# Float16 halves of the attention weights, and probabilities times values as three fp32r products

## What is computed

```python
def _fp8_linear_pertensor(x, wq, w_scale, in_scale):
    xq = _div_clamp_fp8(x, in_scale)          # clip, bf16, then float8 e4m3
    return einsum('bsi,oi->bso', xq * in_scale, wq) * w_scale
def _gqa(q, k, v):                            # q: 16 heads of 128, k and v: 8 groups
    scores = einsum('bsghd,btgd->bghst', q, k) / sqrt(128)
    return einsum('bghst,btgd->bsghd', softmax(scores), v)
...
q, qx = ln(linear(x, wq)), ln(linear(x, wqx))
k, v = ln(linear(x, wk)), linear(x, wv)
kx, vx = split(ctx @ w_kv_x.T); kx = ln(kx)
out = linear(concat(_gqa(q, k, v), _gqa(qx, kx, vx)) * smooth, wproj)
x = x + tanh(g) * out
```

## Time and profile before

| | |
|---|---|
| median of 3 runs | 1677.27 us (1674.27 to 1680.37) |
| profiled execution, span | 1673.7 us; the page gives no other time of it |
| TensorE busy | 1623.2 us, 97% |
| ScalarE busy | 1102.9 us, 66% |
| VectorE busy | 1083.2 us, 65% |
| GpSimd busy | 485.3 us, 29% |
| moved by DMA | 220.7 MB |

### The profile page before, as it was taken

The page is one execution under the profiler, slowest core; times in us unless marked ns, Lnnn a source line. Parts: engine busy times, 40 slices in busy tenths (PEclk is TensorE's granted clock), DMA queues, the critical chain, the costliest instruction groups (busy, mean ns, idle before and its releaser), DMA issues.

```text
span 1673.7 us, 27163 instructions
## 1 busy us (share of the span) xinstructions
PE 1623.2 (97%) x9136; PEld 1335.0 (80%) x9136; DVE 1083.2 (65%) x2115; ACT 1102.9 (66%) x2983; POOL 485.3 (29%) x515
## 2 busy tenths in 40 slices
PE   7989989999999999999999999999999999999998
PEld 6878756666778888888788888888888788887887
DVE  6258855445985767777777776566666666788322
ACT  4364245553559888888888887878778787885100
POOL 1001122224424424334243343342433433330000
PEclk9999989999999999999999999999999999999999
DMA  7031649995772143283342362121152121110011
GB/s 271 26 107 41 258 151 325 311 316 187 243 270 80 54 183 104 92 333 109 113 182 89 133 264 83 57 88 57 57 218 79 44 108 56 38 45 1 25 38 38
DMA packets 75156, 220.72 MB, mean 132 GB/s; under 512 B 6368, under 2 KB 14560, under 8 KB 68640
## 3 DMA queue, kind: packets, MB, share of 16 engines
q1 hardware_dynamic: 69360, 200.61, 33.1%
q0 software_dynamic: 5680, 18.62, 3.6%
HBM read 158.65 MB, written 60.56 MB: 131 GB/s over the span
## 4 chain that ended last, share of the span: by engine, by line
PE 78%; DVE 4%; ACT 4%; issue 1%; DMA 1%; POOL 1%; ACTq 0%; POOLq 0%; SPq 0%; DVEq 0%
PE bank L2478 10%; PE bank L2479 10%; PE bank L97 7%; PE bank L2541 7%; PE bank L99 7%; PE bank L98 7%; PE bank L2559 6%; PE bank L2572 6%; PE bank L2530 5%; PE bank L1388 4%; PE bank L1408 4%; PE bank L2551 3%; PE bank L1368 1%; DVE x_res L1747 1%; ACT t_sc L2699 1%
## 5 line engine op out<-in xcount | busy, mean ns | idle before, releaser
L2810 DVE TENSOR_TENSOR t_hn<-bank,t_rs 128x256 f32<-128x256 f32 (+1 forms) x256 | 130.7, 552 | 140.1 <-POOL t_rs L2443 72.7
L2478 PE MATMUL bank<-t_slot,t_x_q 128*128 128x512 f32 x512 | 205.8, 402 | 0.0
L2440 POOL TENSOR_SCALAR t_ve<-t_ss 128x4 f32<-128x4 f32 (+1 forms) x128 | 25.9, 202 | 616.4 <-DVE t_ss L2806 608.9
L2479 PE MATMUL bank<-t_slot,t_x_q 128*128 128x512 f32 x512 | 200.2, 391 | 0.0
L2699 ACT ACTIVATE t_sc<-bank,t_mx 128x128 f32<-128x128 f32 x512 | 183.9, 455 | 3.5 <-DVE t_mx L2830 3.5
L2443 POOL TENSOR_TENSOR t_rs<-t_ve,t_mhalf 128x4 f32<-128x4 f32 (+1 forms) x128 | 171.0, 1336 | 10.6
L2699 ACT ACTIVATION_READ_ACCUMULATOR t_sc<-bank,t_mx 128x1 f32 x512 | 151.6, 296 | 0.0
L2737 ACT ACTIVATE t_y<-bank,smooth 128x128 bf16<-128x128 f32 x512 | 139.3, 401 | 1.9 <-PE bank L2559 1.9
L2541 PEld LDWEIGHTS bank<-t_hT 128*128 128x128 f32 x1024 | 120.1, 191 | 16.8 <-ACT t_hT L2726 16.2
L2541 PE MATMUL bank<-t_hT 128*128 128x128 f32 x1024 | 131.0, 281 | 2.3 <-ACT t_hT L2726 2.3
L2479 PE MATMUL bank<-t_slot,t_x_kv 128*128 128x256 f32 x512 | 125.6, 283 | 0.0
(11 more groups left out here) (344 smaller groups left out, 4159.1 us busy)
## 6 DMA issues: line engine op xcount, KB each, us to landing
t_slot<-w_ready SPq DMA_DIRECT2D x16, 2048.0 KB, 9.8
t_xh<-xq_scratch SPq DMA_DIRECT2D x64, 512.0 KB, 3.6
t_cr<-in_ctxT_dram SPq DMA_DIRECT2D x64, 256.0 KB, 2.7
y_rows<-s_y SPq DMA_DIRECT2D x39, 256.0 KB, 3.2
e_w<-in_w_units_dram SPq DMA_DIRECT2D x8, 1024.0 KB, 12.4
w_rows<-in_w_qkv_dram SPq DMA_DIRECT2D x8, 1024.0 KB, 6.2
w_ready<-w_hi SPq DMA_DIRECT2D x8, 1024.0 KB, 6.3
w_ready<-w_lo SPq DMA_DIRECT2D x8, 1024.0 KB, 6.1
```

Of the source, the lines that this page charges most:

```text
L2478: nc.tensor.matmul(out, x_in[:, k, :], w[0][:, k, a:b], start=k == 0, stop=False)
L2479: last = nc.tensor.matmul(out, x_in[:, k, :], w[1][:, k, a:b], start=False, stop=k == KT - 1)
L2810: nc.vector.tensor_tensor(hn[:, lo:hi, :], b3[bk][:, 0:hi - lo, :], rs[:, lo:hi].unsqueeze(2).broadcast_to([P, hi - lo, P]), ALU.mult).the ...
```

## The change

Each weight half of the segments q, qx, v and k is stored in float16 (`w_half`), those of the context segment stay float32 (`w_plain`). So that float16 can hold them, each segment is divided by a power of two: `half_constants()` in `Retention` finds it from the scales (an input `scales` of 1 MB is loaded for it), and `env.sigma` keeps the factor that undoes it, which ScalarE applies in the squares, the values and the keys. Queries and keys read the float16 rows `xh` directly, `rows_q` and `rows_kv` go. Probabilities and values get a high half (float32r, by ScalarE as before) and a low half by VectorE (`probs_low`, `values_low`), and `attend` is `three_products`. `w_lo` has one buffer instead of two, and stores are two for each half. The diff, cut to its core:

```diff
 class ReadyWeights:
+    STORED = 32
     def store_hi(self, sp, n):
         sp.dma_start(self.dram[quarter, :, :, 0, k, :].rearrange("s p n -> p s n"),
-                     self.hi[:].bitcast(FP32).rearrange("p (s n) -> p s n", s=4)).then_inc(self.hi_st, 16)
+                     self.hi[:].rearrange("p (s n) -> p s n", s=3)).then_inc(self.hi_st, 16)
+        sp.dma_start(self.dram_plain[quarter, :, 0, k, :], self.hi_rest[:].bitcast(FP32)).then_inc(self.hi_st, 16)
...
+        def half_constants():
+            ins, steps = env.cols("in_scale"), self.halves
+            dve.wait_ge(self.scales_in, 16)
+            v.tensor_reduce(self.most[:], self.scales[:], op=ALU.max, axis=AX.X, apply_absolute_value=True
+                            ).then_inc(steps, 1)
...
         low(2)
+        half_constants()
         added(1)
...
     def sync(sp):
         def x_rows(m):
             if m >= 2:
-                sp.wait_ge(xkv_in, m - 1)
-                sp.wait_ge(xq_in, m - 1)
+                sp.wait_ge(b_ps, (m - 1) * 2)
         def weights(quarter, seg, loaded):
+            home = homes[quarter][seg]
+            if seg == KVX:
+                sp.dma_start(slots[home][:].bitcast(FP32), ready.dram_plain[quarter]).then_inc(loaded, 16)
+            else:
+                sp.dma_start(halves16[home][:], ready.dram[quarter, {KV: 2, WQ_: 0, WQX: 1}[seg]]).then_inc(loaded, 16)
...
     def tensor(pe):
-        def project(out, w, a, b, x_in):
+        def project(out, w, a, b, rows, kind):
             for k in range(KT):
-                nc.tensor.matmul(out, x_in[:, k, :], w[0][:, k, a:b], start=k == 0, stop=False)
-                last = nc.tensor.matmul(out, x_in[:, k, :], w[1][:, k, a:b], start=False, stop=k == KT - 1)
+                nc.tensor.matmul(out, rows[:, k, kind, :], w[0][:, k, a:b], start=k == 0, stop=False)
+                last = nc.tensor.matmul(out, rows[:, k, kind, :], w[1][:, k, a:b], start=False, stop=k == KT - 1)
             return last
...
         def attend(m, par):
             for part in range(2):
-                pe.wait_ge(pt_in, m * 2 + part + 1)
+                pe.wait_ge(ptl_in, m * 2 + part + 1)
                 for g in range(QG):
-                    h = (1 - part) * QH + 2 * g
-                    last = nc.tensor.matmul(bank[6 + part][:, g * 256:(g + 1) * 256],
-                                            vv[par][:, (1 - part) * QG + g, :], pT[:, h:h + 2, :],
-                                            start=True, stop=True)
+                    h, v = (1 - part) * QH + 2 * g, (1 - part) * QG + g
+                    last = three_products(nc, bank[6 + part][:, g * 256:(g + 1) * 256], vv[par][:, v, :],
+                                          vv_lo[par][:, v, :], pT[:, h:h + 2, :], pT_lo[:, h:h + 2, :], True, True)
                 last.then_inc(pv_ps, 1)
...
     def scalar(act):
-        def rows_kv(m, par):
-            nc.scalar.activation(x_kv[:], xh[par][:, :, 2:4, :].rearrange("p k v s -> p v k s"), ACT.Copy
-                                 ).then_inc(xkv_in, 1)
-        def rows_q(m, par):
-            nc.scalar.activation(x_q[:], xh[par][:, :, 0:2, :].rearrange("p k v s -> p v k s"), ACT.Copy
-                                 ).then_inc(xq_in, 1)
...
-                nc.scalar.activation(hn[:, part * QH:part * QH + QH, :], b3[part][:], ACT.Square).then_inc(sqb_in, 1)
+                nc.scalar.activation(hn[:, part * QH:part * QH + QH, :], b3[part][:], ACT.Square,
+                                     scale=env.sigma[:, part:part + 1]).then_inc(sqb_in, 1)
...
     def vector(dve):
+        def values_low(m, par):
+            dve.wait_ge(vcp_in, m * 2 + 2)
+            if later(m, 2):
+                dve.wait_ge(pv_ps, m * 2 - 2)
+            nc.vector.scalar_tensor_tensor(vv_lo[par][:, 0:QG, :], b3[2][:, 2:4, :], env.sigma[:, 3:4],
+                                           vv[par][:, 0:QG, :].bitcast(FP32), ALU.mult, ALU.subtract)
+            nc.vector.tensor_tensor(vv_lo[par][:, QG:2 * QG, :], b3[3][:, 2:4, :],
+                                    vv[par][:, QG:2 * QG, :].bitcast(FP32), ALU.subtract)
+        def probs_low(m):
+            for part in range(2):
+                dve.wait_ge(pt_in, m * 2 + part + 1)
+                if part == 0 and later(m, 1):
+                    dve.wait_ge(pv_ps, m * 2)
+                nc.vector.tensor_tensor(pT_lo[:, side(part), :], b3[6 + part][:], pT[:, side(part), :].bitcast(FP32),
+                                        ALU.subtract).then_inc(ptl_in, 1)
...
             if has(i):
                 normalise_b(i)
+            if has(i - 1):
+                probs_low(i - 1)
             if has(i + 1):
                 sums_a(i + 1)
...
             if has(i + 1):
+                values_low(i + 1, 1 - par)
                 normalise_a(i + 1)
...
         def last_steps():
             normalise_b(M - 1)
             de.x_lo(dve, 0, range(2, KT))
+            probs_low(M - 2)
             rounded(M - 3, 1 - M % 2, 1)
...
             de.h_low(dve, 0, 1)
+            probs_low(M - 1)
             rounded(M - 2, M % 2, 1)
```

More of the change, by code:

```diff
@@ L117, with __init__ @@
     PLAIN = 1536
-    def __init__(self, nc, env, sems, rows, lo, hi, hs, first, last):
+    STORED = 32
+    def __init__(self, nc, env, sems, rows, lo, lo_plain, hi, hi_plain, hs, first, last):
         self.nc, self.env, self.rows, self.lo, self.hi, self.hs = nc, env, rows, lo, hi, hs
-        self.first, self.count, self.dram = first, last - first, env.dram["w_ready"]
+        self.lo_rest, self.hi_rest = lo_plain, hi_plain
+        self.first, self.count = first, last - first
+        self.dram, self.dram_plain = env.dram["w_half"], env.dram["w_plain"]
         (rows_in0, rows_in1, self.summed, self.centred, self.hi_in, self.lo_in, self.hi_st, lo_st0, lo_st1) = sems
@@ L307, in __init__ @@
         self.inv, self.sinv = at("inv", 156.125, [P, 4 * KT]), at("sinv", 156.25, [P, Q * 8])
+        self.scales = at("scales", 160, [P, 4, D])
+        self.most, self.factor = at("most", 156.5, [P, 4]), at("factor", 156.625, [P, 4])
+        self.power, self.inverse = (at(n, 156.75 + i / 8, [P, 4], U32) for i, n in enumerate(("power", "inverse")))
     def sync(self, sp):
@@ L1467, in scalar @@
             if s == SLOTS_N - 3:
-                act.wait_ge(self.ready.hi_st, 16 * self.ready.count)
+                act.wait_ge(self.ready.hi_st, self.ready.STORED * self.ready.count)
                 self.units.hi_part(act, 0)
@@ L2254, in attention @@
     slots = [sb(f"slot{i}", kb, [P, 2, KT, D], F32R) for i, kb in enumerate(SLOTS)]
+    halves16 = [sb(f"half{i}", kb, [P, 2, KT, D], F16) for i, kb in enumerate(SLOTS)]
     slots32 = [sb(f"raw{i}", kb, [P, 2, 4, D]) for i, kb in enumerate(SLOTS)]
@@ L2259, in attention @@
     xh = [sb("xh0", 168, [P, KT, 4, P], F16), sb("xh1", 96, [P, KT, 4, P], F16)]
-    x_q = sb("x_q", 100, [P, 2, KT, P], F32R)
     cr = sb("cr", 104, [P, KT, P])
     sqk = sb("sqk", 106, [P, 2 * QG, P])
-    pT = sb("pT", 108, [P, KH, P])
-    vv = [sb(f"vv{i}", 112 + 2 * i, [P, 2 * QG, P]) for i in range(2)]
+    pT = sb("pT", 108, [P, KH, P], F32R)
+    pT_lo = sb("pT_lo", 100, [P, KH, P], F32R)
+    vv = [sb(f"vv{i}", 112 + 2 * i, [P, 2 * QG, P], F32R) for i in range(2)]
+    vv_lo = [sb(f"vv_lo{i}", 160 + 2 * i, [P, 2 * QG, P], F32R) for i in range(2)]
     y = sb("y", 116, [P, 2, QH * P], BF16)
@@ L2507, in context_keys_values, with queries @@
             last.then_inc(a_ps, 1)
-        def queries(m, quarter):
+        def queries(m, par, quarter):
             if opens(m):
                 pe.wait_ge(q_w, 16 * (m // B + 1))
-            pe.wait_ge(xq_in, m + 1)
             if later(m, 1):
                 pe.wait_ge(e_in, m * 3 - 1)
-            project(bank[0][:], halves(m, quarter, WQ_), 0, D, x_q[:, 0]).then_inc(b_ps, 1)
+            project(bank[0][:], halves(m, quarter, WQ_), 0, D, xh[par], 0).then_inc(b_ps, 1)
             if opens(m):
@@ L2519, in queries @@
                 pe.wait_ge(e_in, m * 3)
-            project(bank[1][:], halves(m, quarter, WQX), 0, D, x_q[:, 1]).then_inc(b_ps, 1)
+            project(bank[1][:], halves(m, quarter, WQX), 0, D, xh[par], 1).then_inc(b_ps, 1)
         def turn(m):
@@ L2589, in step @@
             if has(i + 1):
[L2590 removed]
+                queries(i + 1, 1 - par, quarter)
         def last_steps():
@@ L2935, in vector @@
         sums_a(0)
+        values_low(0, 0)
         normalise_a(0)
@@ L3107, in laid_out @@
         "proj_in_scale")}
+    f["scales"] = np.concatenate([scal(l1[n]) for n in ("q_in_scale", "qx_in_scale", "k_in_scale", "v_in_scale")], 1)
     f["params"] = np.concatenate(
```

173 lines of the change are left out of this document (91 added, 82 removed).

## The result

| | kernel before | changed kernel |
|---|---|---|
| time, median of 4 runs each | 1678.8 us (1674.3 to 1681.2) | 1658.7 us (1657.8 to 1659.6) |
| ratio of the times, 95% interval | | 0.9885 (0.9865 to 0.9904) |
| profiled execution: span | 1673.7 us | 1656.1 us |
| ordinary step, scores to scores | 15.87 us | 15.50 us |
| first scores, last scores (us of the span) | 505.4, 1512.3 | 503.9, 1494.8 |

The changed kernel is faster by 1.15%, 20 us of the medians, 17.6 us of the two spans. The forecast was 1652 us, its range 1635 to 1671; it was made from a median of 1677.3 before, which a fourth run has moved to 1678.8.

What follows compares the result with a forecast made beforehand. TensorE was taken to set the 15.87 us step, with ScalarE's hand-over of hT tight before the scores. Terms -26.9 - 3.1 - 1 + 3.2 + 2.3 = -25.5 from 1677.3 gave 1652 us, range 1635 to 1671.

Steps and rivals of the forecast that it cites:

- Float16 queries, keys and values: TensorE's products in each step: queries save 0.21 us, the 256-column keys and values 0.18, together 0.39.
- Attend: Probabilities times values: 1.74 to 1.43 us, but the 0.31 stays inside the 3.05 that hT needs.
- The first rival: Attend counts as well: if hT is ready earlier, up to 0.28 us more a step, -17, 1635 us; chance 0.11.
- The seam's 0.03: Where scores wait for hT: the seam's 0.05 us minus a start-up, counted as attend's only gain in a step.
- Steps: Attention steps: 15.45 us instead of 15.87, 0.42 less, 64 x 0.42 = -26.9 us.
- steps 1 to 6: Steps carrying rounding pieces on both engines: ScalarE gains what VectorE loses, 0.
- Quarters: Four steps where ScalarE converts wproj, 4 x 1.09 us: its slack grows by a few tenths, -1 us (0 to -2).
- VectorE's loop: VectorE's way through a step with 1.93 us of low halves added: 14.0 to 15.0 us, under the step's 15.45.
- The slower rival: If exponentials start late behind the first maximum, VectorE's loop is 16.38 us, +0.51 a step, 1712 us; chance 0.08.
- Weights at half size: Before the first scores: a store queued behind a 2 MB load lands some 5 us earlier, shortening VectorE's wait: -3.1 us.
- Prologue 0: Start: 1 MB of scales ahead of a_cT must cost less than 5.5 us, otherwise 1 to 3; constants 0.
- Tail: last_steps: attend of the 63rd step waits for late low halves, +3.2 us, then runs at half clock, +2.3.

Runs made afterwards that it cites:

- Run 1: Changed kernel with attend again one float32 product and no low halves, float16 weights and rows kept: 1651.2 us, ratio 0.9848.
- run 2: Changed kernel with the two groups of query heads in the other order, each half of the scores waiting for its own group: 1638.0 us, ratio 0.9768.
- run 8: Kernel before with only the swap of the query heads' groups: 1668.9 us against 1674.6, ratio 0.9964.
- run 7: Changed kernel with one unread VectorE maximum ahead of each of the two subtractions of probs_low: 1675.8 us, ratio 1.0010.
- Run 4: Kernel before with one store of attention input rows issued ahead of the 2 MB weight load, not behind it: 1674.8 us against 1677.5, ratio 0.9984.
- Run 3: Changed kernel with the 63rd step's probs_low and the last normalise_b moved earlier on VectorE in the last steps: 1653.0 us, ratio 0.9849.

## Why the prediction was right, and where it was off

*Float16 queries, keys and values: right.* 0.215 a product was forecast for the queries and 0.2155 came, 0.108 for 256 columns and 0.109 came. The 0.31 behind the first query, which the prediction kept, was a border of records and no cost: that block ends with 0.215 throughout, and the scores' block is 0.08 longer. Net it is 0.22 and 0.16, for 0.21 and 0.18. Run 1 shows the pair by itself: 0.36 a step against 0.39.

*Attend: right.* It was priced at nothing, since the scores wait for the turned heads; runs 1 and 2 show that by taking each side away. The first rival, attend counts as well, needed hT earlier, and run 2 is that case: it is true of the swapped kernel alone. The seam's 0.03 did not come. The prediction had read the scores' wait as 0.05 us at the matmul; it was a wait of the weight load too, and worth 0.12 (run 8). Of that 0.01 lies ahead of the scores and 0.11 in them, so that hand-over and attend did end together, as the prediction read them, but waiting was not free.

*Steps: the mechanism right, the size off.* Forecast 64 x 0.42 = 26.9; measured 0.37 a step, and 21.8 us over the 63 intervals once the tail's 5.8 are set apart. Of the 5 us missing, some 3 are the 0.05 a step. The rest is the sentence on steps 1 to 6, "ScalarE gains what VectorE loses: 0": these steps did not get their share of the 0.4 either. Without the low halves they gained 3.1 us (128.65 to 125.6, run 1), with them 1.7. The low halves also delay the residual on VectorE, for which the second half of the scores waits there, 0.21 us.

*Quarters: off.* -1 was forecast beyond the steps' share, -0.2 came (-2.4 less 6 x 0.37). The step of the conversions gained 0.73 (18.30 to 17.57), 0.36 more than an ordinary one, which over three of them is the forecast 1 us. The one behind it gained hardly anything (15.89 to 15.86), and run 1 gives that back, 15.5. The term had looked at ScalarE alone; what goes with the low halves takes the 1 us back.

*VectorE's loop: right.* 14.0 to 15.0 was forecast; run 7 bounds it by 14.3 in plain steps and puts it near 14.5 with late weights. Its way through the step was met within 0.2 us: exponentials at 2.9 (forecast 2.8), squares at 5.6 (5.5), normalising ended at 11.6 (11.4), low halves at 12.2 and 12.8 (12.0 and 12.6). The slower rival's 16.38 is ruled out, and its condition too: the exponentials start 0.04 us behind the first maximum, not 0.9. L1264 at 0.28 came as foreseen, 0.29 in the mean. The margin was thin: in run 7 another 1.2 us a step cost 21 us, and in the first 8 intervals and the quarters the low halves already cost 2.2.

*Weights at half size: right in size, in part by luck, and poor to see.* -3.1 was forecast. The gap fell from 3.82 to 1.30:

```profile
486.38 0.47 PE L99 MATMUL bank<-t_slot,t_c_hi 128*128 128x512 f32 x1 [1.30 <-DVE x_res L1771]
```

Counted from the product on e_h behind the 1.16 us wait that both profiles have (441.94 before, 444.22 now), TensorE reaches the first scores in 59.7 us instead of 63.5. Of these 3.8 us the gap gave 2.5, not 3.1; behind it the clock is 1.00 from 487 to 490 instead of 0.50, which the prediction had counted for nothing, and gave 1.9; some was lost again before the scores. Up to 444.22 the changed kernel's profile had lost 2.3, which nothing in the change explains (below). Run 4 reaches the same end in another way, 2.8 us by its ratio. Prologue 0: seen neither in a gap nor in a late a_cT.

*Tail: right.* +3.2 for the wait and +2.3 for the clock; 3.34 us, and 5.8 in all. Run 3 takes 5.3 back with two pieces moved.

The sum was -25.5 from 1677.3 and gave 1652; the medians of four runs each give -20.1. Of the miss of 6.7 us 1.5 is the base, which moved to 1678.8, and 5.4 the change. Steps and quarters explain 6.1 of that (27.9 forecast, 21.8 measured): the 0.05 a step, the early steps, and what the step behind the conversions lost. The other terms came within 0.7 us, less than medians of four runs can tell. Every forecast mechanism was found at its place.

## What to carry to other kernels

When a part of a step gets shorter, look first at what else ends at the same moment: here float32 attend and the hand-over of the turned heads ended within 0.12 us of each other (run 8), and shortening one gave nothing until an order that cost nothing let the other go. Low halves and the like that are taken on another engine go directly behind what they are taken from, in the steps written out by hand as well; at the end of the program such a wait is paid in full, and here the lower clock behind it cost 2.5 us on top of 3.3. An engine's room is to be read separately in each kind of step: VectorE had 1.2 us or more in the plain ones and next to none in the first eight.
